# Cross-attention and expert layers: inputs laid out on the host, q, k, v of two tiles in one record, the softmax expansion four steps later

## The reference, cut to what matters

```python
x = x + xattn(layernorm(x), ctx_1024, ctx_1024, ...)   # 32 batches of 128 tokens, 256 channels
x = x + ffn(layernorm(x), ...)

def xattn(q, k, v, ...):
    query, key_p, value = q @ Wq.T + bq, k @ Wk.T + bk, v @ Wv.T + bv
    # reshape(B, -1, 16, 16): per token a 16 x 16 attention between its own 16 heads' rows
    logits = einsum('bsid,bsjd->bsij', query, key_p) / sqrt(16)
    out = einsum('bsij,bsjd->bsid', softmax(logits), value)
    return transpose(out, (0, 2, 1, 3)).reshape(B, -1, 256) @ Wd.T + bd

def ffn(x, w_red, wg, W1, b1, W2, b2):                 # 8 experts, 256 -> 512 -> 256, best one per token
    gates = softmax((x @ w_red) @ normalized(wg).T); idx = argmax(gates); score = max(gates)
    h = gelu(x @ W1[idx] + b1[idx])
    return (h @ W2[idx] + b2[idx]) * score
```

## Time and profile before

| | us |
|---|---|
| median of 3 runs (431.3 to 433.75) | 432.21 |
| the profiled execution | 430.04 |
| its span, first to last instruction | 428.1 |
| mean granted TensorE clock, share of full | 0.979 |
| PE busy (89% of the span) | 381.1 |
| DVE busy (73%) | 310.9 |
| POOL busy (69%) | 297.2 |
| ACT busy (55%) | 234.8 |

### The profile page before, as it was taken

How to read it: one execution, slowest core, us unless ns; L and a number is a source line. 1 busy time by engine, 2 the same in 40 slices (tenths; PEclk the granted TensorE clock), 3 DMA queues, 4 the chain that set the end, 5 groups by cost and what they waited for, 6 DMA issues and landing times.

```text
span 428.1 us, 11390 instructions
## 1 busy us (share of the span) xinstructions
PE 381.1 (89%) x3791; PEld 303.4 (71%) x3791; DVE 310.9 (73%) x667; ACT 234.8 (55%) x783; POOL 297.2 (69%) x399
## 2 busy tenths in 40 slices
PE   6996999999999989998888687978999999999980
PEld 6774676676766657565555466767999999999970
DVE  3746899899998989999999665579456555555640
ACT  4443778787686877776752564571344444444420
POOL 2767678787687877776775964656387777787751
PEclk9999999999999999999999899999899999999996
DMA  7696866978779787886566501131022222222200
GB/s 163 207 264 164 228 173 209 268 193 239 184 211 260 190 229 181 230 209 175 133 155 185 154 27 39 52 116 48 29 64 75 64 75 74 61 69 65 65 17 0
DMA packets 97433, 59.31 MB, mean 139 GB/s; under 512 B 70366, under 2 KB 88447, under 8 KB 97376
## 3 DMA queue, kind: packets, MB, share of 16 engines
q1 hardware_dynamic: 92368, 48.44, 41.8%
q0 software_dynamic: 3744, 9.53, 7.8%
q10 hardware_dynamic: 1264, 0.61, 0.8%
HBM read 37.41 MB, written 22.07 MB: 139 GB/s over the span
## 4 chain that ended last, share of the span: by engine, by line
PE 34%; DMA 24%; DVE 14%; issue 9%; SPq 9%; POOL 7%; ACT 2%; DVEq 1%; ACTq 0%; POOLq 0%
DMA qkv_scr<-qkv 21%; PE bQ L1107 14%; PE bKV L1075 8%; PE bL L1075 7%; SPq L248 4%; POOL kx L374 3%; SPq L252 2%; SPq L283 2%; DMA b2b<-in_L_ffn_wg 2%; DVE qkv L485 2%; PE bT L1089 2%; DVE qkv L492 1%; DMA ql<-qkv_scr 1%; PE bO L1057 1%; POOL r L420 1%
## 5 line engine op out<-in xcount | busy, mean ns | idle before, releaser
L374 POOL TENSOR_TENSOR kx<-ql,mask 128x2048 f32<-128x2048 f32 x32 | 117.6, 3675 | 42.7 <-issue 32.9
L1107 PE MATMUL bQ<-w,wA 128*128 x312 | 74.3, 381 | 3.4 <-DVE r L721 2.8
L475 DVE TENSOR_TENSOR ax<-bA,mask 128x2048 f32<-128x2048 f32 x32 | 73.3, 2290 | 0.6 <-PE bA L1013 0.6
L1107 PEld LDWEIGHTS bQ<-w,wA 128*128 128x128 f32 x312 | 56.2, 190 | 10.6 <-issue 4.5
L924 PE MATMUL bKV<-wA,xcT 128*128 128x512 f32 x128 | 60.2, 593 | 0.0
L397 POOL DMA_INDIRECT out<-r,isc x39 | 41.3, 1059 | 22.3 <-issue 13.4
L420 POOL DMA_INDIRECT r<-row_scr,ig x39 | 40.5, 1038 | 6.0 <-issue 2.4
L862 ACT ACTIVATE wA<-bL,r 128x128 f32<-128x128 f32 x76 | 21.6, 367 | 41.3 <-PE bL L1075 26.7
L862 ACT ACTIVATE wA<-bKV,r 128x128 f32<-128x128 f32 x80 | 22.8, 367 | 36.1 <-issue 18.8
L355 POOL TENSOR_TENSOR rs<-ve,half 128x2 f32<-128x2 f32 x39 | 28.3, 726 | 20.3 <-ACT ve L742 20.2
L932 PE MATMUL bL<-kx,pad 128*32 128x128 f32 x1024 | 35.8, 282 | 6.8 <-POOL kx L374 6.8
(11 more groups left out here) (202 smaller groups left out, 724.5 us busy)
## 6 DMA issues: line engine op xcount, KB each, us to landing
qkv_scr<-qkv SPq DMA_DIRECT2D x32, 384.0 KB, 4.2
ql<-qkv_scr SPq DMA_DIRECT2D x32, 384.0 KB, 4.6
row_scr<-cat SPq DMA_DIRECT2D x32, 133.5 KB, 3.6
w1b<-in_L_ffn_W SPq DMA_DIRECT2D x16, 256.0 KB, 4.5
w<-in_L_ffn_W SPq DMA_DIRECT2D x16, 256.0 KB, 4.7
xt<-in_x SPq DMA_DIRECT2D x15, 256.0 KB, 4.9
ct<-in_ctx SPq DMA_DIRECT2D x15, 256.0 KB, 4.9
b2b<-in_L_ffn_b SPq DMA_DIRECT2D x4, 256.0 KB, 4.7
```

What stands on the lines that cost most here:

```text
L374: eng.tensor_tensor(block(kx[:, z % 2, :]), spread_heads(ql[z % 2][:, :, 0:HD]), mask_b, ALU.mult).then_inc(S["kx"], 1)
L475: eng.tensor_tensor(block(ax[:, :]), spread_heads(bA[:, 0:C].rearrange("p (l i) -> p l i", l=NH)), mask_b, ALU.mult).then_inc(S["ax"], 1)
L1107: i_ = eng.matmul(bQ[:, 0:C], hT[b % 2][:, k, :], w2[:, bass.ds(eb * (KH * C) + k * C, C)], start=(k == 0), stop=(k == KH - 1))
```

## The change

- **Inputs.** The host now lays the tensors out: x in pairs of tiles with each partition's data in one piece, and `xc`, x and ctx already transposed. PE's four input transposes and ACT's copy go; `xcT` is a ring of four tiles in SBUF, loaded by SP. Wk, Wv, Wq, Wd come transposed, W1 with b1 and W2 in one piece per partition. PE multiplies Wq with a matrix of -1/256 for its mean. x itself is still loaded for the residual and the moments.
- **Records.** q, k, v of two tiles share one record. SP stores and loads it in odd steps only. One piece of the load is 96 numbers, where it was 48.
- **Steps.** QK is for s0 = t - 5, PV for s1 = t - 6, the output projection for w = t - 7; kx and pad for t - 4 where it was t - 2, the row store for t - 9. `FIRST`, `LAST` and `ROUTE` move by two steps. Slot 0 gathers one row set, slot 1 two.
- **Expansion.** Up to t = 34 DVE expands four of the eight blocks of ax (three in the routing steps), and ACT the others, one instruction a block with the mask as scale; PV waits for ACT. DVE's order in a step is now maximum, subtraction, expansion, softmax, cat, gm, and the projection's sums last. From t = 35 (`STEADY`) on the turn and the whole expansion for the next step stand inside the slot before: after w1s on DVE, between up and down on PE.
- **Moments.** The gate matrix has a ninth column of -1/256, so bY carries the negative mean of cat; its pass on ACT goes. POOL computes ve from va (one tensor_scalar of 128x2), and its power goes straight into cat.
- **Expert loads** start at step 3, one half a step, two in steps 24 to 28. `fill` is 3 transposes for t < 6.

```diff
-LAST = NT + 6
-FIRST = NT - 1
+LAST = NT + 8
+FIRST = NT + 1
 HOLD = NT - CR
-ROUTE = R1 + 4
+ROUTE = R1 + 6
 SLOTS_AT = {t: (t - FIRST,) for t in range(FIRST, LAST + 1)}
 NEXT = LAST + 1 - FIRST
-HALVES_IN = 0
-DOUBLE = (0, 1)
+HALVES_IN = 3
+DOUBLE = (24, 25, 26, 27, 28)
 MOE = 16 * 4 * NE
 B2_IN = HALVES_IN + 4 * NE - len(DOUBLE)
 B2_PARTS = 4
+SHARE = 4
+STEADY = FIRST + 2
...
-    qkv_scr = nc.dram_tensor("qkv_scr", [NT, P, NH, W3], f32, kind="Internal").ap()
+    qkv_scr = nc.dram_tensor("qkv_scr", [NT // 2, P, NH, 2, W3], f32, kind="Internal").ap()
...
+        def sync_x(eng, n):
+            if n < NT:
+                if n >= XR:
+                    eng.wait_ge(S["x2"], n - XR + 2)
+                eng.dma_start(xt[:, n % XR:n % XR + 2, 0:C], x[n // 2]).then_inc(S[f"ld_x{n // 2 % 3}"], 16)
+
+        def sync_xc(eng, c):
+            if c < NT:
+                if c >= XC:
+                    eng.wait_ge(S["qq"], c - XC + 2)
+                eng.dma_start(xcT[:, c % XC:c % XC + 2, :, :], xc[c // 2]).then_inc(S[f"ld_c{c // 2 % 2}"], 16)
...
+            sync_inputs(eng)
+            for t in range(LAST + 2):
+                p = t // 2
+                if live(t) and t % 2 == 1:
+                    eng.wait_ge(S["qad"], t + 1)
+                    eng.dma_start(qkv_scr[p], qkv[p % 2][:, :, :, :]).then_inc(S[f"st_q{p % 2}"], 16)
+                    sync_xc(eng, t + 3)
+                sync_row(eng, t - 9)
+                if live(t) and t % 2 == 1:
+                    eng.wait_ge(S[f"st_q{p % 2}"], (p // 2 + 1) * 16)
+                    if p > 1:
+                        eng.wait_ge(S["kx"], t - 3)
+                        eng.wait_ge(S["pad"], t - 3)
+                    eng.dma_start(ql[p % 2][:, :, :, :], qkv_scr[p].rearrange("(b l) x w c -> x b l (w c)", b=NB)
+                                  ).then_inc(S[f"ld_q{p % 2}"], 16)
+                    sync_x(eng, t + 5)
...
-                n, v, d, z = t + 1, t - 2, t - 6, t - 2
+                n, v, d, z = t + 1, t - 2, t - 8, t - 4
...
+                    eng.tensor_scalar(ve[:, :], va[:, :], 1.0 / C, EPS, ALU.mult, ALU.add).then_inc(S["ve"], 1)
+                    eng.wait_ge(S["ve"], t + 2)
+                    eng.tensor_tensor(cat[d % CR][:, RS:RX + 1], ve[:, :], half2[:, :], ALU.pow).then_inc(S["rs"], 1)
...
-            for a in (0, 1) if s == 0 else (s + 1,):
+            for a in (0,) if s == 0 else (1, 2) if s == 1 else (s + 1,):
...
+        def shared(s1):
+            return s1 + 6 < STEADY
+
+        def scalar_blocks(s1):
+            if not shared(s1):
+                return 0
+            return SHARE + 1 if ROUTE <= s1 + 6 < ROUTE + 7 else SHARE
+
         def expand(eng, s1):
+            b = scalar_blocks(s1)
             eng.wait_ge(S["tr_a"], s1 + 1)
             if s1 > 0:
                 eng.wait_ge(S["pvo"], s1)
-            eng.tensor_tensor(block(ax[:, :]), spread_heads(bA[:, 0:C].rearrange("p (l i) -> p l i", l=NH)),
-                              mask_b, ALU.mult).then_inc(S["ax"], 1)
+            eng.tensor_tensor(block(ax[:, :])[:, :, b:, :],
+                              bA[:, 0:C].rearrange("p (l i) -> p l i", l=NH).unsqueeze(2).broadcast_to((P, NH, NB - b, HD)),
+                              mask[:, b:].unsqueeze(1).unsqueeze(3).broadcast_to((P, NH, NB - b, HD)),
+                              ALU.mult).then_inc(S["ax0" if b > 0 else "ax"], 1)
...
-                a, s0, s1, w = t, t - 3, t - 4, t - 5
-                if live(s1) and not live(a):
-                    expand(eng, s1)
-                if t < 4:
+                a, s0, s1, w = t, t - 5, t - 6, t - 7
...
+                if live(s1) and t < STEADY:
+                    expand(eng, s1)
+                if live(s0) and t < STEADY:
+                    normed(eng, s0)
...
-                    vector_up(eng, s)
+                    vector_weights(eng, s)
+                    if live(s1 + 1) and t + 1 >= STEADY:
+                        expand(eng, s1 + 1)
+                    vector_turned(eng, s)
...
+            if w == 0:
+                eng.activation(junk[:, 0, :], in_, ACT.Identity, scale=-1.0 / C,
+                               accum_out=nm[:, :]).then_inc(S["nm0"], 1)
+                eng.wait_ge(S["nm0"], k + 1)
+            eng.activation(junk[:, w, :], in_, ACT.Square, bias=nm[:, :] if w == 0 else cat[k % CR][:, EXT - 1:EXT],
+                           accum_out=va[:, 1 - w:2 - w]).then_inc(S[f"va{w}"], 1)
...
+                if live(s1) and shared(s1):
+                    scalar_expand(eng, s1)
...
+        def scalar_expand(eng, s1):
+            eng.wait_ge(S["ax0"], s1 + 1)
+            for b in range(scalar_blocks(s1)):
+                i_ = eng.activation(block(ax[:, :])[:, :, b, :], bA[:, 0:C].rearrange("p (l i) -> p l i", l=NH), ACT.Copy,
+                                    scale=mask[:, b:b + 1])
+            i_.then_inc(S["ax"], 1)
...
-        def tensor_turned(eng, a):
-            if a > 0:
-                eng.wait_ge(S[f"ld_x{a // 2 % 3}"], (a // 6 + 1) * 16)
-                eng.wait_ge(S[f"ld_c{a // 2 % 3}"], (a // 6 + 1) * 16)
-                eng.wait_ge(S["xT"], a)
-            else:
-                eng.wait_ge(S["ld_xx"], 16)
-                eng.wait_ge(S["ld_cc"], 16)
-            for k in range(KC):
-                eng.transpose(bT[:, k * P:(k + 1) * P], xt[:, a % XR, k * P:(k + 1) * P], ident[:, :])
-            for k in range(KC):
-                i_ = eng.transpose(bT[:, (KC + k) * P:(KC + k + 1) * P], ct[:, a % CT, k * P:(k + 1) * P],
-                                   ident[:, :])
-            i_.then_inc(S["tr_in"], 1)
...
+                if t == FIRST + 2:
+                    tensor_rows(eng, 1)
...
+                    if live(s1 + 1) and t + 1 >= STEADY:
+                        tensor_turn(eng, t + 1, s1 + 1)
...
-                    fill(eng, 10, bA)
-                if t == NT + 5:
+                    if s != 1:
+                        tensor_rows(eng, s)
+                if t < 6:
+                    fill(eng, 3, bA)
```

451 lines of the change are left out of this document (191 added, 260 removed).

## The result

| | before | after |
|---|---|---|
| median of 4 runs each, same chip (lowest to highest), us | 432.98 (431.30 to 433.98) | 404.20 (402.80 to 404.92) |
| ratio of the two, 95% interval | | 0.9335 (0.9292 to 0.9378) |
| profiled execution, us | 430.04 | 403.76 |
| its span, us | 428.1 | 401.9 |

The changed kernel is 6.65% faster, 404.2 us where 406.0 was predicted with a range of 392 to 423. The span is 401.9 against a worked-out 401.7. That agreement is partly luck, as the terms will show. First the page of the changed kernel: the engines, the queue of SP's transfers (packets, MB, share of 16 engines), the chain by engine, the group of ACT's blocks, and the transfers with KB of each and us from issue to landing.

The account below looks back on a forecast made before the run. A ring through DRAM (6.68 us a step) and DVE (6.28) were taken to bind almost together. Start 45.3, 17 steps of 6.0, 7 of 6.5, tail to 274.5, slots 127.2: span 401.7, plus 1.94 and 2.17: 405.8; range 392 to 423.

Parts of the forecast that it names:

- PE's step: Middle steps: PE's own work falls from 6.27 without waits to 5.73 us once the four input transposes go.
- DVE, no longer the bound: Middle steps: with half of ax moved away, DVE's work falls from 6.28 to 5.2 us a step.
- The pace: Time per attention step: 6.0 us in the middle, 6.5 in the seven steps taken as routing steps.
- ACT's block: Cost of one 128x256 expansion block on ACT: 0.37 us taken, 0.51 the dearest; four at 1.45 a step.
- a rival ACT: Middle steps: at 0.51 us a block ACT works 5.9 a step and sets the pace; 416 us, chance 0.22.
- the prediction's ring: Old middle steps: kx, QK, DVE, store, load and SP's issue sum to 20.0 us over three steps, 6.66 each.
- the pair's transfers: Store and load of a two-tile record through DRAM: 4.5 and 5.5 us, giving a ring of 5.2 a step.
- the slower rival: Pair's store and load cost double, 8.4 and 9.2 us, so 7.1 a step; 437 us, chance 0.05.
- The first load: Start: the first record is loaded at 28.6 us, so POOL's kx(0) starts then, where it was 23.91.
- The tail: From QK(31) to the pure slots: 53.3 us before, 3 taken off because ax runs under the slot's matmuls.
- Full overlap: Third rival case: everything overlaps, pace 5.73 and 6.25, earlier first load, shorter tail; 394 us, chance 0.13.
- That the ring wasn't the bound before: Old middle steps: if DVE alone was the limit, PE's 5.73 would bind and the time equal Full overlap's.

Follow-up runs that it names:

- b_share: The kernel before with only the sharing added: four blocks of ax on ACT (five in routing steps), DVE's half in its old place; 466.73 us, ratio 1.0846.
- share3: The changed kernel with three blocks of ax on ACT and five on DVE (four and four in routing steps); 401.61 us, ratio 0.9339.

## Why the prediction came out

**What held.** *PE's step.* 5.73 was worked out from the earlier trace rows, 5.76 measured without the wait for ACT and 5.82 with it; its other half, that a step of the old kernel which waits for nothing takes 6.27, is 6.23 in the kernel with the expert half ahead of the load. *DVE, no longer the bound.* Busy 45.34 / 55 x 5.90 = 4.9 a step, where 5.2 was taken; whole, with its gaps, its row is 6.14 to 6.20. *The pace.* 5.90 and 6.49 against 6.0 and 6.5. The 5.90 is fair: 5.82 and one long step. The 6.49 is luck: it was meant for seven routing steps, and is five at 6.60 with two before them that carry no routing (12.44 us, one of them long). *Two more steps of lead cost nothing at the start*: tile 7 at 45.73, predicted 45.3, though not by the way predicted (below). *The slots* are unchanged.

**ACT's block.** The prediction took 0.37 a block with bounds 0.37 and 0.51. Both a low and a high number were right, of different things:

```profile
70.11 1.55 ACT L835 ACTIVATE ax<-bA,mask 128x256 f32<-128x256 f32 x4
```

One block is 0.470 alone, but four take 1.55, so the next begins (1.55 - 0.47) / 3 = 0.36 after the one before. A step pays the 0.36. The Trainium skill (ScalarE: Activation LUTs, Rules for kernel authors) gives about 0.3 us and 0.83 ns an element for one whose bias is a pointer operand, an estimate of 0.51: the record, 0.470, lies nearer to it than to the 0.37 taken, the pitch does not. The row that the prediction set against that rule, L817 with 0.366, has a plain number as its scale and no pointer, so it was no test of it; the blocks have a pointer, as their scale. As a rival ACT lost by the pitch: four blocks at 0.51 each one after the other were to make ACT the bound at 416, and they take 1.45 in the chain. One sign named for that case did show by the letter, PE waiting for ax at PV over 0.3 us a step: the weight loads waited 0.41, but PE's multiplying, still at work on the queries, lost only 0.06 of it.

**Wrong, without effect on the sum: why the old kernel ran at 6.68.** The step that failed is "the ring is worth its sum". Its first paragraph had read the right ring, store, load issued, expert half issued, next store, 7.00 us; then another was summed, and twenty us over three steps came to 6.66. But the order of SP's issues moved 5 us (0.22 a step) while that ring's store and load, 4.3 and 4.6 us from 45 to 165 us, came to 3.7 and 4.8, which is 0.13 a step at the most. What the runs showed in its place are four limits close together: SP's queue at 6.68, the prediction's ring at about 6.4, PE at 6.23 and DVE at 6.14 to 6.20. The change loosens all four, so the forecast came out although it named the wrong one.

**Mis-sized: the pair's transfers.** 4.5 and 5.5 were taken, 5.7 and 6.8 measured, 2.5 more in sum and still under the 17 at which the slower rival starts. The reason given, that most of a transfer's time is queueing behind others, fits one run more (in `b_share`, with a DMA share of 0.70, the same 384 KB landed in 2.9 and 4.4); that the others would come less often doesn't, since the share rose from 0.78 to 0.91 and 0.98. The ring came to 5.6 or, at its worst, 6.2 a step instead of 5.2, which makes one or two steps long and costs about 2 us.

**Mis-sized, and cancelling.** The first load lands 3 us earlier than taken: POOL starts kx(0) at 25.49, predicted 28.6. Nothing came of it by tile 7, for a reason that the prediction didn't have. Two rows of the chain there, and the window behind them:

```profile
29.86 6.78 DMA xt<-in_x
...
40.12 1.94 PE bO L902 x32
...
40.00:45.70 5.70, 5.58 (x70) 4.65 (x71) 2.56 (x6) 1.35 (x4) 5.53 (x5) 0.52 0.97 179
```

The load of x for tiles 8 and 9 stands behind SP's wait for the second store and is issued at 29.86. In step 6 ACT takes the moments of tile 8 first and waits 3.78 us for that load, its blocks of ax stand behind them, and PE idles 4.15 us for them. Then PE works at a granted clock of 0.52, close to the lower of its two levels, 1.2 and 2.4 GHz: PV takes 1.94 where it takes 1.08 at the full clock, and PV, QK, turn and output projection together 5.78 us in the chain where they take 3.21 later. POOL was close behind, busy nearly throughout, with kx at 25.49, 30.80, 36.27 and 41.67: the third was ready at 39.93, when PV began, so without the wait PE could have come to QK up to 2 us sooner by these rows. That is an estimate; no run moves the load. So 45.73 beside 45.3 is luck: 3 us sooner in the first load, and the wait and the low clock against them.

The tail: 3 us were taken for the early expansion, about 6 it is; yet from the end of kx(31), 225.04, to the pure slots it is 49.9 where 50.3 was predicted. The other 3 us went into what the prediction left out: routing pieces that belong to steps 31 and 32, since `ROUTE` moved by two steps, and the extra step. That is argued from the code; no run separates it.

**Rivals.** ACT as the bound at 416 is refuted by its 1.45 us for four blocks and by `share3`. Full overlap (394, pace 5.73) was nearly true in single steps, 5.76 to 5.82, and false in the sum. Doubled transfers need 17 us, 12.5 came in the median and 14.5 at the most in the middle. That the ring wasn't the bound before was nearest to the truth of the rivals, though it was SP's queue and not DVE; its price would have been the third case's, and the time lies between.

## What to carry to other kernels

A term is worth nothing while another limit stands at the same height: undo parts one by one and together, for if both undone cost no more than the dearer one alone (0.962 and 0.962 here), the parts are not two gains that add. Before a ring is believed because its sum fits the pace, follow the chain for several rounds and look at the queue that issues its transfers: what stands behind a wait in an in-order queue is in the ring, and moving one issue ahead of that wait is the cheapest test (-1.1% here, and +2.5% for the load that was put behind it). The same queue cost time at the start of the changed kernel, where a load of x stands behind the wait for a store. Work moved to an idle engine is served where it stands in that engine's queue: the same sharing was worth up to 11 us in the new order and cost 37 in the old.
